# A graph network kernel whose edge attributes are transposed and multiplied with We in the sampling stage of layer 1 instead of in attention

## The reference

```
agg  = segment_sum(h[src], dst)                    # both layers of the first network
h    = h @ W_self + agg / max(deg, 1) @ W_neigh + b
...
e = edge_attr @ We + be                            # (12500, 4 heads, 128)
alpha = (q[dst] * (k[src] + e)).sum(-1) / sqrt(128)
attn  = softmax of alpha over the edges of one target
msg   = (v[src] + e) * attn
out   = segment_sum(msg, dst) + x @ Wskip + bskip
lin   = layernorm(out) @ Wlin + blin
x     = layernorm(x + elu(lin + x))
```

## Time and profile before

| | us |
|---|---|
| median of 3 runs (lowest, highest) | 1772.49 (1771.62, 1773.52) |
| profiled execution | 1765.38 |
| its span on the core | 1763.6 |
| TensorE busy | 1520.7 (86%) |
| VectorE busy | 1254.9 (71%) |
| ScalarE busy | 1125.1 (64%) |
| GpSimd busy | 1044.4 (59%) |

### The profile page before, as it was taken

One profiled execution on the slowest core, in us unless ns is written; L12 is line 12 of the kernel. 1 busy time (PEld: TensorE's weight loads), 2 busy tenths in 40 slices (PEclk: granted clock), 3 DMA queues, 4 the chain that ended last, 5 costly groups with the idle time before them and its releaser, 6 DMA issues. The chain is left out here.

```text
span 1763.6 us, 33507 instructions
## 1 busy us (share of the span) xinstructions
PE 1520.7 (86%) x7745; PEld 1065.6 (60%) x7745; DVE 1254.9 (71%) x6050; ACT 1125.1 (64%) x3051; POOL 1044.4 (59%) x1038
## 2 busy tenths in 40 slices
PE   3599999999999998989455469999999999999992
PEld 2477777777777776777345335555555555555541
DVE  4799999999999996545366545666666666666652
ACT  0499999999999994333144415666666666666672
POOL 4688888868888774653576364555454554545220
PEclk9799999999999999999666699999999999999995
DMA  2366666644444442332121221111111111111000
GB/s 78 108 154 160 154 159 154 156 150 143 148 142 149 141 144 68 84 83 64 30 55 54 58 62 35 38 39 40 38 39 40 38 39 38 40 39 39 15 13 4
DMA packets 124685, 142.48 MB, mean 81 GB/s; under 512 B 32654, under 2 KB 75625, under 8 KB 124574
## 3 DMA queue, kind: packets, MB, share of 16 engines
q1 hardware_dynamic: 97374, 105.01, 19.8%
q0 software_dynamic: 27200, 36.26, 9.0%
HBM read 75.35 MB, written 74.38 MB: 85 GB/s over the span
## 5 line engine op out<-in xcount | busy, mean ns | idle before, releaser
L1227 POOL DMA_INDIRECT out_dram<-big,idx x98 | 99.1, 1011 | 298.4 <-ACT big L1396 159.5
L1210 POOL DMA_INDIRECT big<-x_tab,look x196 | 199.5, 1018 | 92.4 <-issue 61.5
L683 PE MATMUL pb<-MG_s,big 128*128 128x256 f32 x832 | 207.4, 392 | 39.5 <-issue 25.0
L683 PEld LDWEIGHTS pb<-MG_s,big 128*128 128x128 f32 x832 | 149.5, 189 | 141.7 <-issue 79.6
L708 ACT ACTIVATE big<-big 128x128 f32<-128x128 f32 x416 | 170.1, 481 | 0.0
L803 POOL TENSOR_TENSOR big<-big,cl 128x512 f32<-128x512 f32 x104 | 133.3, 1281 | 48.7 <-ACT big L732 41.0
L665 PE MATMUL pb<-C_s,big 128*128 128x128 f32 x832 | 161.9, 276 | 0.0
L666 PE MATMUL pb<-Ws1c_s,big 128*128 128x128 f32 x832 | 161.8, 276 | 0.0
L317 POOL DMA_INDIRECT a_xs<-in_x_dram,idx x98 | 98.8, 1008 | 93.3 <-issue 48.5
L1537 DVE CUSTOM_DVE_ANT_0 big<-pb,big,zero 128x128 f32<-128x128 f32 x392 | 113.9, 346 | 54.2 <-PE pb L1299 53.0
L1038 POOL DMA_INDIRECT big<-h1e_tab,hidx x98 | 102.7, 1048 | 75.1 <-POOLq L1628 33.3
(11 more groups left out here) (339 smaller groups left out, 4016.2 us busy)
## 6 DMA issues: line engine op xcount, KB each, us to landing
big<-in_x_dram SPq DMA_DIRECT2D x104, 256.0 KB
x_tab<-big SPq DMA_DIRECT2D x98, 256.0 KB
out_dram<-big SPq DMA_DIRECT2D x98, 256.0 KB
h1e_tab<-a_rows SPq DMA_DIRECT2D x25, 256.0 KB
x_tab<-a_rows SPq DMA_DIRECT2D x25, 256.0 KB
big<-in_edge_attr_dram SPq DMA_DIRECT2D x97, 64.0 KB
big<-x_tab,look POOLq DMA_INDIRECT x196
dst_row<-in_dst_dram POOLq DMA_DIRECT2D x13, 240.2 KB
```

The costliest lines, as they stand in the source:

```text
L683: t = pe.matmul(o, b_x1T[:, r * P:(r + 1) * P], MG_s[:], start=True, stop=True)
L1210: g.indirect_dma_start(out=o, out_offset=None, in_=x1_tab, in_offset=bass.IndirectOffsetOnAxis(ap=look[:, a, j:j + 1], axis=0), bounds_che ...
```

## The change

In stage c SP now loads the edge attributes in groups of four tiles, TensorE transposes them (new line 1093), ScalarE copies the transposes out (L1123), SP stores them in a table `eT_tab`, TensorE multiplies them with We into two PSUM banks in turn (L1108), ScalarE copies tiles 0 and 2 of the group, VectorE 1 and 3 (`attr_out`, L1140 and L1075), and SP stores these products in `ve_tab` (L1212). In attention SP loads transposes and products back, TensorE has neither the third transpose nor the product with We, and VectorE adds the loaded product to the one with Wv in PSUM (L1608). The wait for the transposes moves to the product with Aqe. The product with Aqk moves ahead of the transposes of c, and VectorE's L1492 (now L1602) behind what were L1500 and L1504. The addition of `crow` moves from stage c to stage a.

```
@@ stage a, VectorE
+                    after(v, "a_yp", s - 1)
+                    v.tensor_tensor(yp, yp, four_rows(crow[:]), ALU.add).then_inc(step("a_yc"), 1)
@@ stage c
+        def attr_out(eng, copy, s, r):
+            t = R * s + r
+            after(eng, f"c_pve{r % 2}", t // 2)
+            landed_before(eng, dma_vs(t % 4), t // 4)
+            copy(c_ve[t % 4][:], VE[r % 2][:]).then_inc(step(f"c_ve{r % 2}"), 1)
@@ TensorE, behind means(s)
+                    pe.wait_ge(dma_ce(s % 2), 16 * loads_of(s))
+                    after(pe, "c_eT", s - 1)
+                    for r in tiles_of(s):
+                        t = pe.transpose(tile_of(TE, r), c_ea[s % 2][:, r, :], ident[:])
+                    t.then_inc(step("c_pea"), 1)
@@ TensorE, behind the product with Wn1
+                if s < NG:
+                    after(pe, "c_eT", s)
+                    for r in tiles_of(s):
+                        after(pe, f"c_ve{r % 2}", (R * s + r) // 2 - 1)
+                        pe.matmul(VE[r % 2][:], c_eT[s % 2][:, r, :], We_s[:], start=True, stop=True).then_inc(step(f"c_pve{r % 2}"), 1)
@@ ScalarE, behind the copy of the means
+                    after(act, "c_pea", s)
+                    after(act, "c_pve1", (R * s) // 2 - 1)
+                    landed_before(act, dma_et(s % 2), s // 2)
+                    act.activation(c_eT[s % 2][:].rearrange("p r d -> p (r d)")[:, 0:n], TE[:, 0:n],
+                                   ACT.Copy).then_inc(step("c_eT"), 1)
@@ ScalarE, behind the normalisation of group s - 2
+                if s < NG:
+                    for r in tiles_of(s)[0::2]:
+                        attr_out(act, lambda o, i: act.activation(o, i, ACT.Copy), s, r)
@@ VectorE
-                    v.tensor_tensor(four(s), four(s), four_rows(crow[:]), ALU.add).then_inc(step("c_yc"), 1)
+                if s < NG:
+                    attr_out(v, v.tensor_copy, s, 1)
...
+                if s < NG and 3 in tiles_of(s):
+                    attr_out(v, v.tensor_copy, s, 3)
@@ SP: store of eT, load of group s + 2, store of x1 of group s - 2, four stores of ve, in this order
@@ attention, SP
-                after(sp, "d_pT", j - 4)
-                sp.dma_start(d_ea[j % 4][0:n, :], edge_attr[j * P:j * P + n, :]).then_inc(dma_ea[j % 4], 16)
+                after(sp, "d_pP", j - 4)
+                sp.dma_start(d_xT[j % XT][:, 2 * D:3 * D], eT_tab[j * P:(j + 1) * P, :]).then_inc(dma_ea[j % 4], 16)
+            def load_values(j):
+                after(sp, "d_vs", j - 4)
+                sp.dma_start(d_ve[j % 4], ve_tab[j * P:(j + 1) * P, :]).then_inc(dma_ve(j % 4), 16)
@@ attention, TensorE
-                    pe.wait_ge(dma_ea[a % 4], 16 * (a // 4 + 1))
-                    for i, s_ in enumerate((d_x1s[a % 4], d_x1d[a % XD], d_ea[a % 4])):
+                    for i, s_ in enumerate((d_x1s[a % 4], d_x1d[a % XD])):
...
-                    pe.matmul(VB[:], X(b, 0), Wv_s[:], start=True, stop=False)
-                    pe.matmul(VB[:], X(b, 2), We_s[:], start=False, stop=True).then_inc(step("d_pV"), 1)
+                    pe.matmul(VB[:], X(b, 0), Wv_s[:], start=True, stop=True).then_inc(step("d_pV"), 1)
@@ attention, ScalarE
-                    act.activation(d_xT[a % XT], TB[:, 0:3 * P], ACT.Copy).then_inc(step("d_xT"), 1)
+                    act.activation(d_xT[a % XT][:, 0:2 * P], TB[:, 0:2 * P], ACT.Copy).then_inc(step("d_xT"), 1)
...
-                    after(act, "d_pV", b)
+                    after(act, "d_vs", b)
@@ attention, VectorE, behind the moved d_nm
+                if live(b):
+                    after(v, "d_pV", b)
+                    v.wait_ge(dma_ve(b % 4), 16 * (b // 4 + 1))
+                    v.tensor_tensor(VB[:], VB[:], d_ve[b % 4], ALU.add).then_inc(step("d_vs"), 1)
```

84 lines of the change are left out of this document (69 added, 15 removed).

## The result

| | before | after |
|---|---|---|
| median of the runs side by side, us | 1773.01 (1771.62 to 1773.59) | 1751.78 (1751.26 to 1753.14) |
| ratio, 95% interval | | 0.9883 (0.9865 to 0.9900) |
| profiled execution, its span, us | 1765.38, 1763.6 | 1751.26, 1749.4 |
| sampling of layer 1: first aggregation to attention's first instruction | 855.4 to 1015.6: 160.2 | 854.6 to 1043.0: 188.4 |
| attention: from there to the end of the span | 748.0 | 706.4 |

The account below looks back on a forecast made before the run. Gathers on GpSimd bound sampling, TensorE attention, where a 6.60 us VectorE-ScalarE ring would take over. 28.1 + 4.3 + 5 + 3 + 0.7 - 24.2 = +16.9 us on 1772.5 gives 1789 us, range 1760 to 1830.

Parts of the forecast that it names:

- The ring's length: Attention: a VectorE-ScalarE cycle of 6.60 us stays, so turns drop only 0.275 us over 88 turns, -24.2 us.
- TensorE alone at 5.905 us: Attention: without the We product and third transpose, TensorE by itself would need 5.905 us a turn instead of 6.875.
- Rival A: Attention: VectorE and ScalarE have slack, so turns reach 5.905 us; 1728 us in total, chance 0.14.
- The addition hidden, 0.69 us: Attention: VectorE's added addition of the stored product takes 0.69 us and fits where VectorE waits for the exponential.
- Rival D: Attention: the addition is stretched to 1.38 us and passes its gap, +23 us, 1812 in total; chance 0.10.
- The pace of a group, 7.0 us, and its path: Layer 1 sampling: a chain of copies, scale, normalisations and products makes groups 7.0 us instead of 5.83, +28.1 us.
- The clock's start, +4.3: Layer 1 sampling: one group runs at half the granted clock, 11.3 us of TensorE work, +4.3 us (0 to 8.6).
- DMA's queueing, +5: Layer 1 sampling: transfers nearly fill the DMA engines, +0.2 us a group, +5 us (0 to +24).
- rival B: Layer 1 sampling: DMA binds, 8.0 us a group, +24 us more, 1808 in total; chance 0.20.
- The end, +3: End of layer 1 sampling: last split, two products, a copy and a store run in sequence, +3 us (1 to 6).
- Crow, +0.7: Stage before: the moved addition of crow delays L942 and L946 by 0.7 us; only the last group shows it.
- rival C: Layer 1 sampling: the clock stays at half, 11.3 us a group, +99 us more, 1888 in total; chance 0.06.

Follow-up runs that it names:

- the fillers: Kernel after plus one unread VectorE comparison per attention turn: ahead of the statistics ratio 1.0220 to before, behind the addition 0.9979.
- the exponential first: Kernel after with ScalarE's exponential of tile d ahead of its copy of the transposes in attention: 1712.83 us against 1766.66 for the kernel before.
- the filler that fits behind it: Kernel after plus one unread VectorE comparison behind the addition in each attention turn: ratio 0.9979 to the kernel before.
- the fastest kernel: Kernel after, attention's exponential ahead of the transposes' copy, sampling's first product copy between scale and normalisations: 1670.91 us against 1730.13 before.

## Why the prediction was wrong

- **The ring's length, the step that failed.** "So the ring itself takes 6.81 - 0.20 = 6.61 us", 6.60 as the mean of the turn less the wait: measured 6.36 (6.37 in the kernel before without the We product) once TensorE was relieved. The difference of 0.24 a turn over 88 turns is 21 us, against the missing 17.4 (the first and last turns gave some back). It was read from a trace in which TensorE set the turn. There only the wait right ahead of the scores counts as slack; stretches inside the ring (L1509 0.35 and L1513 0.40 us on average, 0.29 after) took up slack as well, and came with a position against the gathers that holds only at that turn: L1513 was held in 37 of 80 turns (1100 to 1650 us) before, while in the kernel after L1616 starts up to 0.26 us behind a gather in 79 of 87 turns and is not held once. I had even listed the 0.62 us of L1509 as a collision and left it in. That the mechanism itself, a ring of VectorE and ScalarE that sets the turn once TensorE has less to do, was right is shown by the fillers and by the exponential first.
- **What this step explains.** Of the 31.1 us between +16.9 and -14.2 by the profiles, it is 17.4. With the measured ring and all else as it was, the sum would have been -0.5 us, no change; that the kernel became faster took the terms of the sampling stage too, which were 12.9 us too high (below), and the stage's start (0.8).
- **TensorE alone at 5.905 us**: 5.92 us between 1150 and 1500 us in the fastest kernel, where TensorE is busy throughout: right. **Rival A**, that the ring is no bound and the turn goes to 5.905, did not come; but the turn that it named as deciding, 6.41 us or less, did: 6.36, with the ring still the bound. A ring only 0.24 us shorter than read was enough for that, and 0.14, with 0.08 of the forecast, was too low a chance for this distance.
- **The addition hidden, 0.69 us**: 0.70, hidden, shown by the kernel before without the We product and by the filler that fits behind it. **Rival D**: not seen, the addition's mean is 0.70. That it has one SBUF input and is not held, while L1509 with two is, agrees with the rule of the Trainium skill cited there (SBUF — State Buffer, Who interferes with whom).
- **The pace of a group, 7.0 us, and its path**: 7.03, by the predicted steps. **The clock's start, +4.3**: 22.74 us for the first three groups, +1.6. **DMA's queueing, +5**: nothing; 21 groups without a delay at a share of 0.85 and 271 GB/s (900 to 1000 us), and **rival B** did not come either. The fastest kernel reached 298 GB/s at a share of 0.94 (860 to 990 us). **The end, +3**: 20.2 us behind the last aggregation before, 17.7 after, -2.5; the last products did run behind the last aggregation, but the stage's end before had as much to wait for. **Crow, +0.7**: can't be told apart, the stage began 0.8 us earlier.
- **The clock, rival C**: did not come: 0.98 over the stage.
- The base: the pace of before, 5.83 us, is itself a mean over groups delayed by late gathers. Where these are absent it is 5.39, and the stage costs 39.5 us, close to the 41.1 predicted, but by another sum.

## What to carry to other kernels

A ring beside a full engine can't be measured by subtracting the wait in it: until the engine is relieved, slack hides as stretched instructions, so take each step at its undisturbed duration. When an instruction that waits is moved ahead, count everything that comes to stand behind it, on its engine and on those that wait there; the same copy cost 33 us ahead of the scale and gained 17 behind it. A filler of known length, once in the ring and once in its gap, tells in one comparison what bounds a turn.

## What the runs showed of the hardware

I count over all 20 traces, 1100 to 1650 us, what VectorE did inside a GpSimd indirect DMA (1.0 us); an instruction is called held if it took over 0.05 us more than undisturbed. L1513 (two SBUF inputs, 0.29 us), started 0.35 to 0.60 us behind the DMA's start, was held in 321 of 329 cases, and L1509, also with two, started 0.30 to 0.46 us behind in 83 of 92; held ones nearly always ended within 0.06 us of the DMA's end, which makes them 0.65 us long at most. The comparison L1504 was held in all 110 cases at 0.54 to 0.70 us, and in 28 of 237 earlier than that (0.27 to 0.53). Within the first 0.26 us none of 1135 was held, and of L1500 and the addition L1608, which read PSUM and SBUF, L1500 never was and L1608 stayed at 0.70 us, but for two of 525 (0.82 and 0.83). L1509 started at 0.47 us or later was mostly not held in the kernels with the exponential first; why, no run shows. A GpSimd addition of 128x128 held even a 128x1 instruction, which started 0.06 us behind it (0.37 us instead of 0.16). L1504 reads one tensor and a column of numbers, so two tensor inputs are not the whole condition. The rule of the Trainium skill cited in the prediction (SBUF — State Buffer, Who interferes with whom) is for instructions outside the two-port modes, and no row tells whether L1504 ran in one. Between the two sorts of measurement the kernel before differs by 35 to 44 us, 12 of them in layer 1's sampling stage; the stage of the kernel after is 188 us in either.
